# Setting up layer 0 of a four-layer graph network: row statistics of x taken earlier, squared norms split over two engines, the row table stored in seven parts

## The reference, cut to what matters

```python
h = jnp.maximum(_layernorm(x, axis=-1), 0.0)      # 6250 x 256
# inside layer 0, for every edge: logmap(h[src], h[dst]); it needs
_sqnorm(h)                                        # sum of squares of each row of h
agg = jax.ops.segment_sum(msg, dst, num_segments=N)
```

## Time and profile before

| | us |
|---|---|
| median of 3 runs | 5282.82 |
| the 3 runs | 5282.82, 5283.91, 5278.07 |
| the profiled execution's own time | 5278.94 |
| its span in the trace | 5277.1 |
| mean granted clock of TensorE in it | 0.805 of full speed |

### The profile page before, as it was taken

The page is one execution under the profiler, slowest core; times in us unless marked ns, Lnnn a source line. Parts: engine busy times, 40 slices in busy tenths (PEclk is TensorE's granted clock), DMA queues, the critical chain, the costliest instruction groups (busy, mean ns, idle before and its releaser), DMA issues. The chain is left out here.

```text
span 5277.1 us, 59132 instructions
## 1 busy us (share of the span) xinstructions
PE 3291.6 (62%) x11741; PEld 2264.1 (43%) x11741; DVE 3440.5 (65%) x10607; ACT 1850.3 (35%) x4402; POOL 3348.5 (63%) x3529
## 2 busy tenths in 40 slices
PE   3388887888543566566564566656662566666667
PEld 2266665666332333333333344434441344444445
DVE  4299999999994666666667555555557455555555
ACT  0555555555684333333335333333336000000001
POOL 0377777777004777777761777777771677777773
PEclk8599999999776777777877888888886777777788
DMA  2454555554114444444435555555554544444443
GB/s 79 113 132 133 133 133 133 135 133 119 49 35 127 107 107 107 107 107 107 107 86 168 131 134 134 132 131 134 134 132 142 138 114 113 114 113 114 106 107 99
DMA packets 302414, 617.14 MB, mean 117 GB/s; under 512 B 66553, under 2 KB 175093, under 8 KB 302070
## 3 DMA queue, kind: packets, MB, share of 16 engines
q0 software_dynamic: 168960, 467.01, 33.9%
q1 hardware_dynamic: 107766, 117.55, 7.4%
q10 hardware_dynamic: 25344, 28.85, 2.1%
HBM read 560.58 MB, written 52.57 MB: 116 GB/s over the span
## 5 line engine op out<-in xcount | busy, mean ns | idle before, releaser
L457 POOL DMA_INDIRECT X<-table,src_tab x2640 | 2499.3, 947 | 1396.4 <-issue 752.7
L562 PE MATMUL psum<-X,onehot 128*128 128x259 f32 x5280 | 1824.7, 489 | 1001.1 <-ACT onehot L699 326.2
L1106 DVE SCALAR_TENSOR_TENSOR A<-A,same_tab,psum 128x259 f32 x3476 | 1670.4, 481 | 799.9 <-PE psum L562 564.3
L562 PEld LDWEIGHTS psum<-X,onehot 128*128 128x128 f32 x5280 | 1162.3, 239 | 1459.2 <-ACT onehot L699 562.1
L447 POOL DMA_INDIRECT X<-table,src_tab x880 | 836.9, 951 | 348.3 <-issue 251.3
L699 ACT ACTIVATE onehot<-G,zero_col,ecols 128x128 f32<-128x128 bf16 x1760 | 727.0, 481 | 701.0 <-PE psum L562 460.2
L571 PE MATMUL psum<-H,G 128*128 x1760 | 605.4, 431 | 314.2 <-DVE G L1194 195.5
L551 PE MATMUL psum<-X,onehot 128*128 128x259 f32 x1760 | 568.4, 408 | 4.3 <-DVE A L1106 2.2
L571 PEld LDWEIGHTS psum<-H,G 128*128 128x128 f32 x1760 | 326.5, 207 | 491.2 <-issue 451.8
L699 ACT ACTIVATE onehot<-onehot,zero_col,coef 128x128 f32<-128x128 bf16 x880 | 365.8, 481 | 128.3 <-DVE coef L1237 107.0
L1194 DVE SCALAR_TENSOR_TENSOR G<-psum,X 128x257 f32<-128x257 f32 x880 | 365.7, 417 | 64.0 <-DMA X<-table,src_tab 39.7
(11 more groups left out here) (324 smaller groups left out, 2863.4 us busy)
## 6 DMA issues: line engine op xcount, KB each, us to landing
X<-table,src_tab POOLq DMA_INDIRECT x3520, 2.8
plain<-rows_dram SPq DMA_DIRECT2D x110, 256.0 KB, 3.5
plain<-rows_dram ACTq DMA_DIRECT2D x176, 160.0 KB, 3.5
table<-H SPq DMA_DIRECT2D x21, 906.5 KB, 7.7
x_dram<-X SPq DMA_DIRECT2D x21, 896.0 KB, 4.2
X<-x_dram SPq DMA_DIRECT2D x14, 896.0 KB, 11.2
X<-in_x SPq DMA_DIRECT2D x2, 6144.0 KB
table<-H SPq DMA_DIRECT2D x1, 6345.5 KB, 27.2
```

Source lines behind the costliest of these rows:

```text
L457: pool.indirect_dma_start(ring[:, s % SLOTS, :], None, table, bass.IndirectOffsetOnAxis(src_tab[:, s:s + 1], 0)).then_inc(sem(f"batch_in{s ...
L562: pe.matmul(psum[:, k % ACC_BANKS, 0:W], hots[:, k % HOTS, :], ring[:, k, :], start=True, stop=True).then_inc(sem("used"), 1)
L1106: stt(total, total, same, psum[:, t % ACC_BANKS, 0:W], ALU.mult, ALU.add).then_inc(sem("sum_added"), 1)
```

## The change

Five things change, all ahead of the first gather of layer 0:

1. DVE's statistics of x (49 `bn_stats`, the short operations, the reciprocal and the shift) are moved ahead of its wait for `tables_summed`. They are written out and no longer a loop.
2. ACT's normalizing waits for `rstd_ready` and `tables_summed`. It writes blocks 0 to 41 of H (FREE = 10929 // 259 = 42) at once; blocks 42 to 48 lie over `row_a` and `row_b`, which are moved to the end of H, and wait for `rows_kept`.
3. The squares are shared: ACT does blocks 0 to 20 (X2_ACT = 21; the first 7 before it waits for `rows_kept`, the other 14 after blocks 42 to 48 are normalized), DVE does blocks 21 to 48 after `rows_kept`. Both write the sum straight into AUX2 of H. DVE fills AUX and AUX3 first (`aux_kept`).
4. SP stores the table in seven parts, in the order 0, 3, 1, 4, 2, 5, 6, each when its squares are there.
5. DVE copies AUX2 to the column `x2` afterwards. The counts of `table_stored` in all later waits are adapted.

```diff
@@ tiles
+        ROWS_AT = NB * W - 2 * S - 2
+        row_a, row_b = h_flat[0:1, ROWS_AT:ROWS_AT + S + 1], h_flat[0:1, ROWS_AT + S + 1:ROWS_AT + 2 * S + 2]
+        FREE = ROWS_AT // W
@@ SP, after its 16 transfers
-            store_table(0)
+            for c in (0, 3, 1, 4, 2, 5, 6):
+                if c * UN < X2_ACT:
+                    sp.wait_ge(sem("x2_act"), (c + 1) * UN)
+                    sp.wait_ge(sem("aux_kept"), 1)
+                else:
+                    sp.wait_ge(sem("x2_dve"), (c + 1) * UN - X2_ACT)
+                store_part(c)
@@ POOL
-            pool.wait_ge(sem("table_stored"), 16)
+            pool.wait_ge(sem("table_stored"), 16 * OUTER)
             gathers_layer0()
@@ ACT
+            def norm_first(b):
+                func(H[:, b, 0:D], X[:, b, :], ACT.Relu, bias=col("nmr")[:, b:b + 1],
+                     scale=col("rstd")[:, b:b + 1]).then_inc(sem("normed_first"), 1)
+            def square_first(b):
+                act.wait_ge(sem("normed_first"), b + 1)
+                if b >= UN:
+                    act.wait_ge(sem("x2_act"), b - UN + 1)
+                func(vT[:, b % UN, :], H[:, b, 0:D], ACT.Square, accum_out=H[:, b, AUX2:AUX2 + 1]).then_inc(sem("x2_act"), 1)
             rstd(0)
-            relu_norm(0)
-            square_sums(H, "x2", "h_ready", OUTER, "x2_ready")
+            act.wait_ge(sem("rstd_ready"), 1)
+            act.wait_ge(sem("tables_summed"), 1)
+            for b in range(FREE):
+                norm_first(b)
+            for b in range(UN):
+                square_first(b)
+            act.wait_ge(sem("rows_kept"), 1)
+            for b in range(FREE, NB):
+                norm_first(b)
+            for b in range(UN, X2_ACT):
+                square_first(b)
@@ DVE, between weights_kept and tables_summed
+            dve.wait_ge(sem("x_in"), 32)
+            for b in range(NB):
+                ins = dve.bn_stats(out=stats[:, b, 0:6], in_=X[:, b, :])
+            chain(ins)
...
+            dve.wait_ge(sem("std_ready"), 1)
+            chain(dve.reciprocal(col("rstd"), col("std")))
+            stt(col("nmr"), mv[:, :, 0], -1.0, col("rstd"), ALU.mult, ALU.mult).then_inc(sem("rstd_ready"), 1)
+
             dve.wait_ge(sem("tables_summed"), 1)
@@ DVE, after rows_kept
-            dve.wait_ge(sem("x_in"), 32)
-            layernorm(0)
-            dve.wait_ge(sem("x2_ready"), 1)
             dve.memset(H[:, :, AUX], -0.5)
-            dve.memset(H[:, :, AUX3], 0.0)
-            chain(dve.tensor_copy(H[:, :, AUX2], col("x2")))
-            dve.sem_inc(sem("rows_ready"), 1)
+            chain(dve.memset(H[:, :, AUX3], 0.0))
+            dve.sem_inc(sem("aux_kept"), 1)
+            for b in range(X2_ACT, NB):
+                dve.wait_ge(sem("normed_first"), b + 1)
+                if b >= X2_ACT + UN:
+                    dve.wait_ge(sem("x2_dve"), b - X2_ACT - UN + 1)
+                stt(junk[:, b % UN, :], H[:, b, 0:D], 1.0, H[:, b, 0:D], ALU.mult, ALU.mult,
+                    accum_out=H[:, b, AUX2:AUX2 + 1]).then_inc(sem("x2_dve"), 1)
+            dve.wait_ge(sem("x2_dve"), NB - X2_ACT)
+            dve.wait_ge(sem("x2_act"), X2_ACT)
+            chain(dve.tensor_copy(col("x2"), H[:, :, AUX2]))
...
-            dve.wait_ge(sem("table_stored"), 16)
+            dve.wait_ge(sem("table_stored"), 16 * OUTER)
             dve.tensor_copy(H[:, :, AUX], col("x2")).then_inc(sem("own_squares"), 1)
```

More of the change, by code:

```diff
@@ L63 @@
 HOTS0 = 8
+X2_ACT = 3 * UN
 LAND = 4
@@ L244, in gnn_program @@
         o += 8 * D
-        row_a, row_b = h_flat[0:1, o:o + S + 1], h_flat[0:1, o + S + 1:o + 2 * S + 2]
-        assert o + 2 * S + 2 <= NB * W and EC * S + S <= NB * W
+        ROWS_AT = NB * W - 2 * S - 2
+        row_a, row_b = h_flat[0:1, ROWS_AT:ROWS_AT + S + 1], h_flat[0:1, ROWS_AT + S + 1:ROWS_AT + 2 * S + 2]
+        FREE = ROWS_AT // W
+        assert o <= FREE * W and EC * S + S <= NB * W and X2_ACT <= FREE
         FULL = (ET - 1) // P
@@ L344, in _ @@
             sp.dma_start(X[0:TAIL, NB - 1, :], x[(NB - 1) * P:N, :]).then_inc(sem("x_in"), 16)
-            def store_table(layer):
-                sp.wait_ge(sem("rows_ready"), layer + 1)
-                sp.dma_start(table.rearrange("(b p) w -> p b w", p=P), H[:, :, :]).then_inc(sem("table_stored"), 16)
             def store_part(c):
@@ L462, in _ @@
             pool.memset(A[:, :, :], 0.0).then_inc(sem("sums_zero"), 1)
-            pool.wait_ge(sem("table_stored"), 16)
+            pool.wait_ge(sem("table_stored"), 16 * OUTER)
             gathers_layer0()
             for q in range(3):
-                pool.wait_ge(sem("table_stored"), 16 + 16 * OUTER * (q + 1))
+                pool.wait_ge(sem("table_stored"), 16 * OUTER * (q + 2))
                 gathers(q)
@@ L672, in plain_sums @@
             def plain_sums():
-                pe.wait_ge(sem("table_stored"), 16 + 16 * 3 * OUTER)
+                pe.wait_ge(sem("table_stored"), 16 * 4 * OUTER)
                 for i in range(TURNS):
@@ L780, in weighted @@
                 if q == 1:
-                    act.wait_ge(sem("table_stored"), 16 + 16 * 2 * OUTER)
+                    act.wait_ge(sem("table_stored"), 16 * 3 * OUTER)
                     for first in range(SUBS):
@@ L857, in norm_and_turn @@
                         root_part(n, b // UN + 1)
-            sq = [0]
-            act.sem_inc(sem("sq_turn"), 1)
             rstd(0)
-            relu_norm(0)
-            square_sums(H, "x2", "h_ready", OUTER, "x2_ready")
+            act.wait_ge(sem("rstd_ready"), 1)
[9 more added lines that the diff above has]
+                square_first(b)
             def asked(n):
@@ L1024, in _ @@
             ins.then_inc(sem("weights_kept"), 1)
+            dve.wait_ge(sem("x_in"), 32)
+            for b in range(NB):
+                ins = dve.bn_stats(out=stats[:, b, 0:6], in_=X[:, b, :])
+            chain(ins)
+            m0, m1, v0, v1 = stats[:, :, 1], stats[:, :, 4], stats[:, :, 2], stats[:, :, 5]
+            tt(col("t0"), m0, m1, ALU.add)
+            tt(col("t1"), v0, v1, ALU.add)
+            chain(tt(col("t2"), m0, m1, ALU.subtract))
+            ts(mv[:, :, 0], col("t0"), 0.5, None, ALU.mult)
+            chain(stt(col("t2"), col("t2"), 0.25, col("t2"), ALU.mult, ALU.mult))
+            stt(mv[:, :, 1], col("t1"), 1.0 / D, col("t2"), ALU.mult, ALU.add).then_inc(sem("var_ready"), 1)
+            dve.wait_ge(sem("std_ready"), 1)
+            chain(dve.reciprocal(col("rstd"), col("std")))
+            stt(col("nmr"), mv[:, :, 0], -1.0, col("rstd"), ALU.mult, ALU.mult).then_inc(sem("rstd_ready"), 1)
             dve.wait_ge(sem("tables_summed"), 1)
@@ L1072, in _ @@
             dve.sem_inc(sem("rows_kept"), 1)
[L1074 to L1088, removed]
             def compare(out_, first, n, numbers=None):
```

## The result

The changed kernel took 5218.26 us (4 runs, 5216.86 to 5225.38) against 5283.14 us for the kernel before (4 runs, 5278.07 to 5283.91, three of them those of the table above). The ratio is 0.9883, with a 95% interval of 0.9870 to 0.9897: faster, by 64.9 us. The prediction on record is 5218, with 64.9 us off.

A forecast was written before the change was run, and what follows sets the result against it. No engine alone bounds the run; the setup relay sets layer 0's start. First gather 205.86 to 141.0, 64.9 us off 5278.94, gives 5214.0, or 5217.9 against the median 5282.82; predicted 5218, range 5208 to 5232.

The forecast's parts named there:

- POOL's free pace: Layer 0's gathers: 1.256 us each against 1.25 unheld, independent of start; the end gains what the first gather gains.
- Part 1, the statistics: DVE's statistics run from 44.0 to 64.9 under the matmuls, 11.5 us before 76.40; cost on the path 0.
- the upper bound of 8 us: DVE's written-out statistics loop: at most 0.49 us an operation in place of 0.33, 8 us more, inside the 11.5.
- Parts 2 and 3, normalizing and squares: ACT normalizes 42 blocks in 20.7 us, then waits 4.6; DVE's 28 squares, 0.35 us each, end at 115.3.
- The hold by POOL: DVE's squares after 114.6 might wait until 125.3, the end of POOL's clearing of A; last part ready by 127.8.
- Part 4, the store: SP issues the first table part at 112.8; seven parts take 27.5, small transfers' tail 0.7; first gather 141.0.
- A: Rival, table store: each part pays its landing in line, 13 us more, 5231; chance 0.06.
- the estimate of 12 us more: Table store: each further part pays the Trainium skill's fixed 2.0 us per transfer in line, 12 us more.
- B: Rival, table store: the queue moves parts faster than one transfer, 18.2 us, up to 9.3 less, 5209; chance 0.05.
- C: Rival, DVE's statistics: their cover fails, all 20.9 us come back, 5239; an ineffective change would look alike; chance 0.03.
- D: Rival, table store: seven parts run one after another at 16.0 us each, 112 in all, 5302, slower; chance 0.02.
- E: Rival, layers: a granted clock 10% lower for PE eats the 65 us saved, near 5283; chance 0.02.

The follow-up runs named there:

- early_parts: Changed kernel with parts 0, 1 and 2 normalized and squared first by ACT and stored before the 16 small transfers: 5204.09 us, ratio 0.9857.
- third group: Four runs on another chip: the kernel before (6008.59 us), the changed kernel (5950.25), it with 16 transfers merged into 6 (5940.52), that plus early-stored parts and two-input copy (5936.77).
- before_again: The kernel before, unchanged, run once more for a second profile: 6008.59 us, ratio 1.0.
- few_transfers: Changed kernel with the 16 small transfers ahead of the table merged into 6: 6018.96 us, ratio 0.9884 to the kernel before.
- copy_two_inputs: Changed kernel with DVE's copy of the x2 column written as a maximum of the column with itself: 6018.38 us, ratio 0.9882 to the kernel before.
- after_again: The changed kernel, run once more for a second profile and a tighter ratio: 5215.31 us, ratio 0.9881 to the kernel before.
- one_store: Changed kernel with the table stored as one transfer in place of seven parts, when all squares are there: 5218.19 us.
- stats_late: Changed kernel with the statistics of x put back behind the table work (`rows_kept`): 5253.52 us, ratio 0.9952 to the kernel before.
- early_few: early_parts with the 16 small transfers merged into 6 and DVE's x2 copy written as a two-input maximum: 6016.08 us, ratio 0.9887 to the kernel before.

## Why the prediction was right, point by point

**What bounds it.** SP's wait of 65.7 us was nearly the whole of what this change could gain, with the store still behind the 16 transfers: it went out 64.3 us earlier. It was no bound on the setup: early_parts took another 11.2 us off. That the layers move along was right, but the reason given for it, POOL's free pace, was narrower than the fact. In the third group POOL did not run at that pace: the kernel before spent 1517.9 - 204.0 us on 880 gathers there, 1.49 us each, and the gain still came through. The gathers of layer 0 in before_again (ns of one: least, median, most; first and last start):

```profile
L447 POOL DMA_INDIRECT X<-table,src_tab x880: 940/946/1166, 204.0 to 1517.9; - x176
```

**Part 1, the statistics.** Right: 43.79 to 63.5, against 44.0 to 64.9. The written out loop took 16.11 us against 16.10; the upper bound of 8 us was not needed. The cover left 13.4 us, not 11.5: nothing held the short operations under the matmuls, and the table work behind it started 0.5 us later (76.94 for 76.40). `rows_kept` came 0.9 us later. The 112 matmuls took 43.93 us for 43.24, and the four of L501 behind them 3.09 for 2.77. The statistics beside them are not what did it: with the same statistics the 112 took 43.07 us in early_parts and 43.18 in few_transfers, and without them 44.02 in before_again, where the granted clock was 0.50 (1.2 GHz) from 33 to 37 us. In the first profiles of both kernels it was 1.00 (2.4 GHz) there, so those 0.7 us stay unexplained.

**Parts 2 and 3, normalizing and squares.** 42 blocks in 20.75 us against 20.7, ACT's wait 5.08 against 4.6, DVE's squares 0.35 us apart and done at 116.5 against 115.3. The hold by POOL that I had priced for the squares did not happen, and the row it was read from was misread. L1082 has two SBUF inputs, a form that no later run shows held; it stood behind L1081, which has one, began 0.10 us before it and ended with the clearing:

```profile
122.53 2.78 DVE L1081 TENSOR_SCALAR mv<-cols 128x49 f32<-128x49 f32 x1
```

The same operation took 0.19 us in the changed kernel, away from the clearing, and few_transfers showed nine squares running freely beside it. The hold did strike the copy after the squares, 9.92 us, which fell under "or, if it is held until 125.3". The cover there was the table's own 27 us, and copy_two_inputs showed that removing the hold leaves the first gather where it was.

**Part 4, the store.** The first part went out at 114.10, not 112.8: 0.9 us from `rows_kept`, 0.4 from one of the 16 issues that took 0.86 in place of 0.43. SP waited 2.2 us in all for squares, and the store took no longer for it than one transfer does. From the first issue to the first gather it took 27.4 us, as read off layer 1; the 0.7 for the tail of the small transfers was not needed. So 1.3 us too early and 0.7 too much nearly cancelled, 141.5 against 141.0.

**The sum.** 64.9 us forecast; 64.9 between the medians, 64.3 between first gathers, and after_again gave 63.9 us in its group. That the medians agree to the tenth is luck; the scatter of either kernel is several us.

**The rivals.** A, landing paid part by part: refuted by one_store, and by the pair of 24.6 and 24.4 us in the third group; with it falls the estimate of 12 us more. B, a faster queue: 26.5 us at best in the first two groups and 24.4 in the third, where the single transfer was as fast, no sign of 18.2. C: the cover stood. Its price of 20.9 us is not tested: with statistics that come late but stay ahead of the table work, the normalizing would still run under that work, and no run does this. stats_late is the other case that C named, a change that does not do what it says. That would have cost some 38 us and not 20.9, near 5255 and not 5239, since the normalizing comes back behind the table work with the statistics. So 20.9 was mis-sized for that case. D: the seven parts overlapped. E: looked alive in the first profile (5082.1 us behind the first gather) and died in the second (5071.7); the granted clock was 0.805 and 0.807 in the two, 0.805 in the kernel before.

## What to carry to other kernels

Work that waits only for an input can go under an earlier wait of its engine, and its consumers' work comes along: price the whole train, not the block that is moved. After such a move look at what the queue itself still has in front of the transfer; here 16 small issues of 0.47 us each were next, and storing three parts before them took another 11 us off (5204.09 against 5215.31). The store cut into seven parts of 906.5 KB cost nothing that could be measured on this queue, and it let parts be late by as much as the queue held: squares that ended 10 us later moved the first gather by 2.8 us.

## What the runs showed of the hardware

- A DVE copy of 49 or even of 2 numbers a partition took 9.92, 6.90 and 6.40 us beside GpSimd's clearing of 12691 numbers, always until that ended, and 0.20 us (49 numbers) after it; a `tensor_scalar` of 49 numbers took 2.78 us for 0.19. Squares and a maximum with two SBUF inputs ran at 0.35 and 0.24 us beside it, and so did `bn_stats`, with one input, at 0.33 us: one SBUF input alone does not make the hold.
- Seven parts of 906.5 KB reached their readers in 26.5 to 27.6 us, one transfer of the same bytes in 26.6 and 27.4; in the third group it was 24.4 and 24.9 for the parts and 24.6 for the one. SP needed 13.9 to 15.1 us to issue the seven, with single issues of up to 3.7 us. In early_few, three parts some 7 us apart and four at some 2.3 us, no issue took over 0.38 us.
- The same kernel took 5279 us in one group of runs and 6008 and 6086 in two others, with the same setup to within 2 us, and a mean granted clock of 0.80 to 0.81 in the first and of 0.75 to 0.76 in the others. The lower clock goes with it; that it is the cause was not shown.
